# Maxima 11 instead of 13 steps ahead of the scores in a fused attention and mixture-of-experts layer

## Chip, cores and metric

The kernel runs on one core of one Trainium2 chip. Time is the device time of that core in microseconds (us), the median of several executions. Engines: PE (TensorE), DVE (VectorE), ACT (ScalarE), POOL (GpSimd) and SP (SyncE, which here issues DMAs).

## What is computed

Four batches of 1024 tokens with 128 channels pass through four residual blocks: a rotation with a code book (`_L0_attn_a_ref`), a mixture of experts, attention with 16 heads, and the mixture of experts again. The change lies in the attention and in the routing of the last block:

```python
def _mha(x, Wq, bq, Wk, bk, Wv, bv, Wo, bo):
    ...
    scores = jnp.einsum('bhsd,bhtd->bhst', q, k) / jnp.sqrt(jnp.asarray(D, x.dtype))
    w = jax.nn.softmax(scores, axis=-1)
    o = jnp.einsum('bhst,bhtd->bhsd', w, v)
...
    logits = jnp.einsum('btd,ed->bte', x, router_w)
    top_vals, top_idx = jax.lax.top_k(logits, K)
    ...
    out = jnp.einsum('nk,nkd->nd', w_f, y_sel)
...
    x = x + _L0_ffn_ref(_layernorm(x, axis=-1), ...)
    x = x + _L0_attn_b_ref(_layernorm(x, axis=-1), ...)
    x = x + _L0_ffn_ref(_layernorm(x, axis=-1), ...)
```

A head has 8 channels; the experts are 8, of which each token uses 2.

## The kernel before

The attention works on 16 groups: group G is batch b = G // 4 and four of its heads, g = G % 4. A group has 16 steps, so a score step s from 0 to 255 is G = s // 16, kk = s % 16. In a score step PE multiplies one tile of 128 keys with half of the queries (512) for four heads (`scores`, L2182), ACT takes the exponentials (L1195), and PE multiplies them with the values (`times_values`, L2223).

The softmax needs each query's largest score before the exponentials. It is found by a first pass over the same scores with keys and queries exchanged: in each step of maxima PE makes four products (`first_pass`, L2195) and DVE reduces them two at a time (`maxima`, L1710, two instructions a step). After 8 steps of maxima one half of a group's queries is complete. `merge_maxima` (L1722, L1724) combines and transposes them, POOL negates them and splits them in two parts (`minus_max`, L785 to L787), and SP stores them to DRAM and loads them into two rows of Q (`shift_queries`, L530 and L535), so that the second product already has its maximum subtracted. A half's first scores wait for that load (`q_shifted`).

The maxima run AHEAD = 13 steps ahead: in loop step s every engine does the maxima of step s + AHEAD and the scores of step s. The loop starts at s = -13 with maxima alone and its last 13 steps have scores alone. A half's maxima are complete, and merged, in the step with (s + AHEAD) % 16 equal to 7 or 15.

All engines follow an order written out by hand. PE, for one step: side work for ACT (`fill_for_act`), values, scores and first pass interleaved. PSUM banks pass between the engines in an order fixed by `bank_order`: three for ACT (`act_banks`) and two double banks for the maxima. Beside the main work, steps have side tasks fixed by G and kk:

- g = 2, kk 0, 2, 6, 8: projections of the next batch, which POOL splits (`split_out`) and SP stores and loads;
- g = 0 and 1, kk 10: a normalised block of a coming batch (`norm_block`, POOL, L730) is transposed by PE (L1842);
- kk 3: the finished group's output is transposed (L2144) and normalised by DVE (`normalise`, L1730, L1732);
- for batches 0 and 1, groups 5 to 7 and 9 to 11 also prepare the routing of the last block. POOL sums the LayerNorm statistics of the first half of a batch (`early_stats(b, 0)`) and of its second half (`early_stats(b, 1)`, L846 to L855, ends in tile ve). DVE waits for both at g = 1, kk 15, before `scale_piece` (L1212 and following).

POOL's order within a group G is also fixed:

```python
minus_max(G, 1)
...
if g < 2 and b < B - 1:
    norm_block(2 * b + 2 + g)
...
if 1 <= b <= EARLY and g == 1:
    early_stats(b - 1, 0)
early_sends(2 * (G - 2 * NG))
if G + 1 < GROUPS:
    minus_max(G + 1, 0)
if g < 2 and b < B - 1:
    low_part(2, 2 * b + 2 + g)
    bias_block(2 * b + 2 + g)
...
elif 1 <= b <= EARLY and g == 1:
    early_stats(b - 1, 1)
```

In group 0 eight gathers of expert results (L653) stand between `minus_max(0, 1)` and `norm_block(2)`.

In the last group (G = 15) no maxima are left after its third step, and batch 2 is routed there by `routed_late`: rows normalised by DVE, transposed by PE, router product, two largest, ranks, places, weights. From step LATE (kk 6 of the last group) ACT has a fourth bank. When attention ends, the experts of the last block start, and POOL scatters and gathers token rows (L644, L653).

Of the kernel before, what the change touches and what calls it, by code (L numbers as in the profile page):

```python
# [64 lines left out]
PAIRS = -(-RT // 2)  # L65

GROUPS = B * NG
AHEAD = 13
EARLY = 2
STEP0, STEP1 = -AHEAD, GROUPS * STEPS  # L70
ACT_BANKS = 3
# [28 lines left out]
def max_task(s):  # L100

    G, kk = divmod(s, STEPS)
    if G < 0:
        return None
    b, g = divmod(G, NG)
    if kk == 12 and G == GROUPS - 1:
        return "half", 0
    if kk == 3 and G:
        return "out", G - 1
    if g == 0 and b > 0 and kk in (13, 14):  # L110
        return "wo", b - 1, kk - 13
    if g == 2 and 1 <= b <= EARLY and kk == 15:
        return "logits", b - 1
    if g == 3 and 1 <= b <= EARLY and kk == 9:
        return "rank", b - 1
    return None


def bank_order():

    AR, DR = {}, {}
    for s in range(STEP0, STEP1):
# [5 lines left out]
        for i in range(2):  # L128
            if i == 1 and max_task(s):
                DR[max_task(s)] = len(DR)  # L130
            if s < STEP1 - AHEAD:
                DR["max", s, i] = len(DR)
# [3 lines left out]
def hybrid_layer(nc, a, out):  # L136
    AR, DR = bank_order()
    ctx = ExitStack()
    with ctx:
# [221 lines left out]
        def beside_index(f, b):  # L361

            return B + b - EARLY if f else b

        def rows_known(f, b, u):

            if f and b < EARLY:
                return G_("rows_early"), 2 * b + u + 1
            return G_("rows_ready"), 2 * (beside_index(f, b)) + u + 1
# [29 lines left out]
        def max_taken(*key):  # L399
            return G_("max_taken"), DR[key] + 1  # L400
# [13 lines left out]
        def rows_bank(f, b):  # L414

            return six[:, 3, :] if f and b < 3 else misc[:]

        def route_bank(f, b):
            return six[:, 0, :] if f == 0 and b == 0 else s1[:, 1, :]
# [555 lines left out]
        def _(act):  # L975
# [76 lines left out]
            def rows_out(f, b, u):  # L1052

                act.wait_ge(G_("rows_turned"), 2 * beside_index(f, b) + u + 1)
                if f or b:
                    act.wait_ge(G_("lgs_done"), beside_index(f, b))
                act.activation(hfs[:, u * BLK:(u + 1) * BLK], rows_bank(f, b), ACT.Copy).then_inc(G_("rows_stored"), 1)

            def second_weight(f, b):
                act.wait_ge(G_("d2_ready"), sparse_index(f, b) + 1)  # L1060
                act.activation(ed2[:], d2[:], ACT.Exp).then_inc(G_("ed2_ready"), 1)
# [72 lines left out]

            def routed_late(kk):

                if kk in (7, 8):
                    rows_out(1, 2, kk - 7)
                elif kk == 13:
                    second_weight(1, 2)  # L1140

            def attention_end(e):
# [65 lines left out]
        def _(dve):  # L1208
# [240 lines left out]
            def batch_top_two(f, b, parts=(0, 1, 2)):  # L1449
                if 0 in parts:  # L1450
                    if f:
                        dve.wait_ge(G_("places_early"), EARLY)
                    dve.wait_ge(G_("lgs_done"), beside_index(f, b) + 1)
                    link(dve.tensor_copy(lgb[:], route_bank(f, b)[:, 64:64 + TPB * E]
                                         .rearrange("p (t e) -> p t e", e=E)))
                    largest_two()
                if 1 in parts:
                    link(chosen_two())
                if 2 in parts:
                    mark_two().then_inc(G_("both_ready"), 1)  # L1460
# [23 lines left out]
            def batch_weights(f, b):  # L1484
                dve.wait_ge(G_("ed2_ready"), sparse_index(f, b) + 1)
                link(dve.tensor_scalar(eds2[:], ed2[:], 1.0, None, ALU.add))
                link(dve.reciprocal(pw[:, b, 0, :], eds2[:]))
                ins = dve.tensor_tensor(pw[:, b, 1, :], ed2[:], pw[:, b, 0, :], ALU.mult)
                if f == 0 and b >= 2:
                    ins.then_inc(G_("weights_ready"), 1)  # L1490
                else:
                    link(ins)

            def batch_places(f, b, parts=(0, 1)):

                if 0 in parts:
                    first_lines(f, b)
                if 1 in parts:
                    line_places(b)
# [73 lines left out]
            def rows(f, b):  # L1573
                if f == 0:
                    dve.wait_ge(G_("x1_ready"), 2 * b + 2)
                rows_stats(b, 0)
                link(rows_stats(b, 1))
                rows_scale()
                for u in range(2):
                    rows_apply(f, b, u)  # L1580
# [98 lines left out]

            def routed_late(kk):  # L1680

                if kk == 3:
                    dve.wait_ge(G_("rows_early"), 2 * EARLY)
                    rows(1, 2)
                elif kk == 8:
                    batch_top_two(1, 2)
                elif kk == 11:
                    batch_places(1, 2)
                elif kk == 13:
                    batch_weights(1, 2)  # L1690

            def attention_end(e):
# [13 lines left out]
            def maxima(s, i):  # L1706

                t, th = divmod((s + AHEAD) % STEPS, 2)
                dst = mxp[:, th, t, 0:HG:HG - 1] if i else mxp[:, th, t, 1:HG - 1]
                dve.reduce_max(dst, taken_slot("max", s, i).rearrange("p (a n) -> p a n", a=2),  # L1710
                               AX.X).then_inc(G_("max_taken"), 1)

            def merge_maxima(s, half):

                n = 2 * ((s + AHEAD) // STEPS) + half
                dve.wait_ge(*max_taken("max", s, 1))
# [91 lines left out]
            for s in range(STEP0, STEP1):  # L1808
                G, kk = divmod(s, STEPS)
                b, g = divmod(G, NG)  # L1810
                first = (s + AHEAD) % STEPS
                if s < STEP1 - AHEAD:
                    maxima(s, 0)
# [24 lines left out]
        def _(pe):  # L1838
# [97 lines left out]
            def turn_rows(f, b, u):  # L1936

                n = 2 * beside_index(f, b) + u
                pe.wait_ge(*rows_known(f, b, u))
                if u or b:  # L1940
                    pe.wait_ge(G_("rows_stored"), n)
                for i in range(TPK):
                    ins = pe.transpose(rows_bank(f, b)[:, i * P:(i + 1) * P], hbs[:, b, TPK * u + i, :], ident)
                ins.then_inc(G_("rows_turned"), 1)

            def router(bank, rows, first=0, last=TPB):
                for i in range(first, last):
                    ins = pe.matmul(bank[:, i * E:(i + 1) * E], rows[:, i * P:(i + 1) * P], rwf[:], start=True, stop=True)  # L1948
                return ins

            def batch_router(f, b, halves=(0, 1)):
                for u in halves:
                    pe.wait_ge(G_("rows_stored"), 2 * beside_index(f, b) + u + 1)
                    if u == 0 and (f or b):
                        pe.wait_ge(G_("dest_ready"), beside_index(f, b))
                    elif u == 0:
                        pe.wait_ge(G_("t_ready"), 1)
                    ins = router(route_bank(f, b)[:, 64:64 + TPB * E], hfs, TPK * u, TPK * (u + 1))
                if u:
                    ins.then_inc(G_("lgs_done"), 1)  # L1960
# [9 lines left out]
            def batch_rank(f, b, parts=(0, 1)):  # L1970
                if 0 in parts:
                    pe.wait_ge(G_("both_ready"), beside_index(f, b) + 1)
                    if f == 0 and b == 0:
                        pe.wait_ge(G_("tri_ready"), 1)
                ins = rank_lines(route_bank(f, b)[:, 128:128 + (TPB + 1) * E], parts)
                if 1 in parts:
                    ins.then_inc(G_("rank_done"), 1)
# [122 lines left out]

            def routed_late(kk):

                if kk == 6:
                    pe.wait_ge(*max_taken("max", STEP1 - AHEAD - 1, 1))
                if kk in (6, 7):
                    turn_rows(1, 2, kk - 6)
                if kk in (7, 8):
                    batch_router(1, 2, (kk - 7,))
                elif kk in (10, 11):
                    batch_rank(1, 2, (kk - 10,))  # L2110

            def attention_end(e):

# [44 lines left out]
            def free_bank(*key):  # L2158
                n = AR[key]
                if n == late_first:  # L2160
                    pe.wait_ge(*max_taken("out", GROUPS - 2))
                if n > late_first:
                    pe.wait_ge(G_("act_taken"), n - LATE_BANKS + 1)
                elif n >= ACT_BANKS:
                    pe.wait_ge(G_("act_taken"), n - ACT_BANKS + 1)
                return act_bank(n)
# [211 lines left out]
```

## Time and profile before

| | |
|---|---|
| median of 3 runs | 1103.66 us (1101.62 to 1105.91) |
| profiled execution | 1099.18 us, its span 1097.4 us |
| mean granted TensorE clock | 0.914 |
| PE, DVE, ACT, POOL busy | 84%, 81%, 67%, 44% of the span |
| first maxima, first exponential | 245.87 us, 283.82 us |
| last maxima end, last exponential ends | 907.40 us, 942.98 us |

The attention phase is the stretch from about 246 to 943 us. Times in the trace count from the first instruction. In the timelines a row gives start, duration, engine, line, operation, output and inputs, the number of instructions merged, and in brackets the engine's idle time just before with what ended it.

### The profile page before, as it was taken

The numbers are of one execution on the slowest core, as the hardware profiler recorded it, in microseconds if no ns is written. First come the engines' busy times: TensorE is split into PE (matmuls) and PEld (weight loads), VectorE is DVE, ScalarE is ACT, GpSimd is POOL, SyncE is SP. The second block draws the span as 40 slices with busy tenths as digits, with TensorE's granted clock in tenths as the row PEclk, the third lists the DMA queues.
The fourth block names the chain that finished last, engine by engine and source line by source line (L and its number), as shares of the span: only waits on it lengthen the run. The fifth ranks groups of instructions, "written<-read, shape, count | busy, mean of one in ns | idle before, by whom it ended". The sixth has DMA issues, their size and how long they took to land.

```text
span 1097.4 us, 23130 instructions
## 1 busy us (share of the span) xinstructions
PE 922.2 (84%) x8466; PEld 524.6 (48%) x8466; DVE 890.4 (81%) x1870; ACT 732.3 (67%) x1453; POOL 477.9 (44%) x703
## 2 busy tenths in 40 slices
PE   2862889855899999999999999999999999999650
PEld 1352889852334434443444443443444434699650
DVE  6478768639999999999989999989999994578342
ACT  3232355430599989889887989887889998645320
POOL 3026676655655556116501416631411211526674
PEclk9865899975699999999999999999999998999885
DMA  7351445472100222100221200131110001246452
GB/s 242 108 175 46 131 124 167 136 266 101 42 18 5 78 82 82 42 3 5 73 87 42 85 8 10 66 108 46 54 45 8 15 8 51 73 117 169 139 152 66
DMA packets 96497, 89.80 MB, mean 82 GB/s; under 512 B 17021, under 2 KB 79616, under 8 KB 96258
## 3 DMA queue, kind: packets, MB, share of 16 engines
q1 hardware_dynamic: 88194, 71.54, 20.6%
q0 software_dynamic: 8192, 16.79, 5.3%
q8 instruction: 69, 1.13, 0.4%
q14 instruction: 42, 0.34, 0.1%
HBM read 44.98 MB, written 43.25 MB: 80 GB/s over the span
## 4 chain that ended last, share of the span: by engine, by line
PE 37%; DVE 32%; POOL 10%; issue 8%; ACT 6%; DMA 5%; SPq 1%; DVEq 0%; POOLq 0%; ACTq 0%
DVE mxp L1710 23%; PE acc L2223 12%; PE six L2182 8%; POOL xs L644 4%; ACT PB L1195 3%; POOL hbs L653 3%; PE misc L2182 3%; PE six L2012 2%; DMA hbs<-yd,dest 1%; PE six L2195 1%; PE six L2144 1%; PE acc L2207 1%; PE six L1948 1%; DMA SC<-yd,dest 1%; ACT SC L1182 1%
## 5 line engine op out<-in xcount | busy, mean ns | idle before, releaser
L1710 DVE TENSOR_REDUCE mxp<-six 128x2 f32<-128x1024 f32 x512 | 589.2, 1214 | 26.6 <-PE six L2195 25.4
L1195 ACT ACTIVATE PB<-six 128x512 f32<-128x512 f32 x688 | 388.7, 598 | 52.3 <-PE six L2182 29.2
L2223 PE MATMUL acc<-PB,Vg 128*32 128x256 f32 x3920 | 316.2, 394 | 15.0 <-ACT SC L1182 15.0
L2195 PE MATMUL six<-K,Q 32*128 32x512 f32 x1024 | 265.3, 517 | 27.3 <-DVE mxp L1710 16.8
L2182 PE MATMUL six<-Q,K 32*128 32x512 f32 x688 | 275.5, 503 | 0.0
L1195 ACT ACTIVATE PB<-misc 128x512 f32<-128x512 f32 x336 | 201.0, 598 | 58.3 <-PE misc L2182 39.3
L2182 PEld LDWEIGHTS six<-Q,K 32*128 32x128 f32 x688 | 110.9, 185 | 150.1 <-ACT PB L1195 82.7
L2182 PE MATMUL misc<-Q,K 32*128 32x512 f32 x336 | 168.4, 501 | 0.0
L644 POOL DMA_INDIRECT xs<-hbs,dest x128 | 127.0, 992 | 77.7 <-DVE dest L1520 40.4
L2223 PEld LDWEIGHTS acc<-PB,Vg 128*32 128x32 f32 x3920 | 78.3, 108 | 134.2 <-issue 79.3
L1086 ACT ACTIVATE PB<-PB 128x512 f32<-128x512 f32 x96 | 58.6, 612 | 101.2 <-DVE PB L1548 100.1
L785 POOL TENSOR_SCALAR shifts<-mxt 128x32 fp32r<-128x32 f32 x32 | 9.4, 293 | 266.2 <-DVE mxt L1724 264.6
L2195 PEld LDWEIGHTS six<-K,Q 32*128 32x128 f32 x1024 | 97.8, 189 | 45.0 <-DVE mxp L1710 33.6
L1548 DVE TENSOR_SCALAR PB<-six 128x512 f32<-128x512 f32 x96 | 63.4, 665 | 67.6 <-PE six L2012 66.9
L653 POOL DMA_INDIRECT hbs<-yd,dest x96 | 92.0, 959 | 54.6 <-issue 46.9
L2012 PE MATMUL six<-VH,stage 128*128 128x128 f32 x736 | 102.2, 283 | 0.3 <-issue 0.3
L2182 PEld LDWEIGHTS misc<-Q,K 32*128 32x128 f32 x336 | 61.7, 184 | 67.7 <-ACT PB L1195 34.6
L2012 PEld LDWEIGHTS six<-VH,stage 128*128 128x128 f32 x736 | 93.6, 198 | 1.0 <-issue 0.5
L2027 PE MATMUL acc<-w2s,PB 128*128 x384 | 53.7, 286 | 2.4 <-ACT PB L1086 2.4
L2027 PEld LDWEIGHTS acc<-w2s,PB 128*128 128x128 f32 x384 | 49.7, 202 | 2.6 <-issue 2.6
L1564 DVE COPY stage<-w1s 128x256 f32 x184 | 46.6, 312 | 5.2 <-issue 3.6
L2027 PE MATMUL six<-w2s,PB 128*128 x352 | 46.9, 275 | 1.4 <-ACT PB L1086 1.4
(328 smaller groups left out, 988.8 us busy)
## 6 DMA issues: line engine op xcount, KB each, us to landing
yd<-PB SPq DMA_DIRECT2D x40, 256.0 KB
kq<-parts SPq DMA_DIRECT2D x16, 512.0 KB, 2.9
K<-kq SPq DMA_DIRECT2D x16, 512.0 KB, 3.7
Q<-kq SPq DMA_DIRECT2D x16, 512.0 KB, 4.6
xs<-turned SPq DMA_DIRECT2D x4, 1472.0 KB, 12.1
K<-xs SPq DMA_DIRECT2D x20, 256.0 KB, 4.5
Q<-xs SPq DMA_DIRECT2D x20, 256.0 KB, 4.0
kq<-parts SPq DMA_DIRECT2D x16, 256.0 KB, 3.5
```

The lines of the kernel that those rows point to most:

```text
L644: pl.indirect_dma_start(xs[b], bass.IndirectOffsetOnAxis(ap=dest[:, b, k, i:i + 1], axis=0), hbs[:, b, i, :], None).then_inc(G_(f"sent{b}{ ...
L653: pl.indirect_dma_start(lines_back[b][:, k, i, :], None, yd[b], bass.IndirectOffsetOnAxis(ap=dest[:, b, k, i:i + 1], axis=0)).then_inc(G_( ...
L1086: act.activation(sqs[:, n % 3, 0:w], rls[:, n % 2, 0:w], ACT.Square).then_inc(G_("sqp_done"), 1)
L1195: act.activation(PB[:, s % 3, j, :], scores, ACT.Exp).then_inc(G_("act_taken"), 1)
L1548: dve.tensor_scalar(rls[:, n % 2, 0:w], big[:, n % 3, 0:w], 0.0, None, ALU.max).then_inc(G_("rlp_done"), 1)
L1564: ins = dve.tensor_copy(stage[:, n % STAGED, i, :], w1s[:, ds(at, HID)])
L1710: dve.reduce_max(dst, taken_slot("max", s, i).rearrange("p (a n) -> p a n", a=2), AX.X).then_inc(G_("max_taken"), 1)
L2012: ins = pe.matmul(big[:, n % 3, at:at + P], stage[:, group % STAGED, r % TG, c * P:(c + 1) * P], hTs[:, group % 2, r % TG * P:(r % TG + 1) ...
L2027: ins = pe.matmul(result_bank(group)[:, r % TG * D:(r % TG + 1) * D], sqs[:, n % 3, at:at + P], w2f[:, ds(expert_at[b, r] + c * D, D)], st ...
L2182: pe.matmul(bank, K[rows, G % NG, t * P:(t + 1) * P], Q[rows, G % NG, u * BLK:(u + 1) * BLK], start=True, stop=True).then_inc(G_("act_fill ...
L2195: ins = pe.matmul(slot[:, c * BLK:(c + 1) * BLK], Q[rows, G % NG, t * P:(t + 1) * P], K[rows, G % NG, th * BLK:(th + 1) * BLK], start=True ...
L2223: ins = pe.matmul(acc[RB * j:RB * (j + 1), n], Vg[:, G % 2, t, j, :], PB[:, s % 3, j, n], start=(t == 0 and half == 0), stop=(t == TPB - 1 ...
```

## The change

AHEAD goes from 13 to 11. Each merge then happens two score steps later (kk 4 and kk 12 instead of kk 2 and kk 10), the loop begins at s = -11, and its last 11 steps have no maxima. Each piece of batch 2's routing in the last group moves one step later, on all engines. The first use of the fourth ACT bank, which lies in the maxima's banks, waits for the last maxima instead of for the output of group 14.

```diff
-AHEAD = 13
+AHEAD = 11
...
-                if kk in (7, 8):
-                    rows_out(1, 2, kk - 7)
-                elif kk == 13:
+                if kk in (8, 9):
+                    rows_out(1, 2, kk - 8)
+                elif kk == 14:
                     second_weight(1, 2)
...
-                if kk == 3:
+                if kk == 4:
                     dve.wait_ge(G_("rows_early"), 2 * EARLY)
                     rows(1, 2)
-                elif kk == 8:
+                elif kk == 9:
                     batch_top_two(1, 2)
-                elif kk == 11:
+                elif kk == 12:
                     batch_places(1, 2)
-                elif kk == 13:
+                elif kk == 14:
                     batch_weights(1, 2)
...
-                if kk == 6:
+                if kk == 7:
                     pe.wait_ge(*max_taken("max", STEP1 - AHEAD - 1, 1))
-                if kk in (6, 7):
-                    turn_rows(1, 2, kk - 6)
                 if kk in (7, 8):
-                    batch_router(1, 2, (kk - 7,))
-                elif kk in (10, 11):
-                    batch_rank(1, 2, (kk - 10,))
+                    turn_rows(1, 2, kk - 7)
+                if kk in (8, 9):
+                    batch_router(1, 2, (kk - 8,))
+                elif kk in (11, 12):
+                    batch_rank(1, 2, (kk - 11,))
...
                 if n == late_first:
-                    pe.wait_ge(*max_taken("out", GROUPS - 2))
+                    pe.wait_ge(*max_taken("max", STEP1 - AHEAD - 1, 1))
```

## Rows read from the trace of the kernel before

**Rows 1.** The page: span, then busy us, share and instructions of engines.
```profile
span 1097.4 us, 23130 instructions
...
PE 922.2 (84%) x8466; PEld 524.6 (48%) x8466; DVE 890.4 (81%) x1870; ACT 732.3 (67%) x1453; POOL 477.9 (44%) x703
```

**Rows 2.** Stretches of the attention phase, columns in the first line.
```profile
core 0: us, PE busy (x) PEld busy (x) DVE busy (x) ACT busy (x) POOL busy (x), PEclk, DMA share, GB/s
257.80:283.80 26.00, 13.46 (x36) 4.91 (x36) 25.35 (x53) 0.00 (x0) 12.49 (x17) 0.50 0.12 31
862.50:900.40 37.90, 36.65 (x400) 15.29 (x392) 37.73 (x39) 34.77 (x67) 6.28 (x11) 1.00 0.04 11
...
523.10:569.40 46.30, 44.19 (x430) 19.40 (x428) 40.68 (x52) 38.68 (x73) 16.40 (x25) 0.97 0.26 95
...
924.70:934.90 10.20, 10.20 (x44) 3.31 (x43) 3.57 (x33) 5.99 (x12) 0.00 (x0) 0.50 0.01 2
```

**Rows 3.** Timeline of all engines, 850 to 862 us: merge to first scores.
```profile
851.18 0.21 DVE L1724 STREAM_TRANSPOSE mxt<-mxc 128x32 f32<-128x32 f32 x1
...
851.32 11.36 DVE L1710 TENSOR_REDUCE mxp<-six 128x2 f32<-128x1024 f32 x10
...
852.20 0.29 POOL L787 TENSOR_SCALAR shifts<-mxr 128x32 fp32r<-128x32 f32 x1
...
852.51 0.52 SPq L530 DMA_DIRECT2D shift<-shifts  x1
...
854.55 1.04 SPq L535 DMA_DIRECT2D Q<-shift  x2
...
861.70 0.47 PE L2182 MATMUL misc<-Q,K 32*128 32x512 f32 x1
```

**Rows 4.** Timeline of ACT in the last group: exponentials on bank misc.
```profile
909.83 0.59 ACT L1195 ACTIVATE PB<-misc 128x512 f32<-128x512 f32 x1
...
914.68 0.60 ACT L1195 ACTIVATE PB<-misc 128x512 f32<-128x512 f32 x1
```

**Rows 5.** Chain of waits, 505 to 530 us (start, us, what).
```profile
511.24 0.22 DVE mxt L1724
...
512.54 1.24 POOL hTl L680
513.78 1.24 POOL x L738
515.01 0.70 POOL turned L846
...
523.42 0.21 POOL ve L855
523.65 0.18 DVE rs L1212
```

**Rows 6.** Timeline of DVE, 516 to 534 us: group 5, kk 15.
```profile
523.65 0.17 DVE L1212 TENSOR_SCALAR rs<-ve 128x8 int32<-128x8 int32 x1 [0.61 <-POOL ve L855]
```

**Rows 7.** Timeline of DVE, 683 to 698 us: group 9, kk 15.
```profile
693.81 0.17 DVE L1212 TENSOR_SCALAR rs<-ve 128x8 int32<-128x8 int32 x1 [0.62 <-POOL ve L855]
```

**Rows 8.** Timeline of PE, 516 to 534 us.
```profile
525.94 0.50 PE L2195 MATMUL six<-K,Q 32*128 32x512 f32 x2 [0.23 <-DVE mxp L1710]
```

**Rows 9.** Timeline of all engines, 302 to 310 us: a block is normalised and transposed.
```profile
302.73 3.14 POOL L730 TENSOR_SCALAR hb<-x,mv,rs 128x128 f32<-128x128 f32 x4
...
309.20 0.66 PE L1842 MATMUL six<-cst,hb 128*128 128x128 f32 x4
```

**Rows 10.** Stretches around a pause of PE after the attention phase.
```profile
1018.00:1020.40 2.40, 0.14 (x2) 0.00 (x0) 0.87 (x4) 1.12 (x2) 1.79 (x3) 0.99 0.16 55
1020.40:1027.40 7.00, 0.00 (x0) 0.00 (x0) 0.00 (x0) 0.00 (x0) 5.17 (x7) 0.50 0.35 107
1027.40:1030.60 3.20, 3.19 (x15) 3.19 (x16) 0.33 (x1) 0.60 (x1) 2.39 (x3) 0.50 1.04 273
```

**Rows 11.** Timeline of POOL, 955 to 982 us: the first gather of the last block.
```profile
979.74 1.00 POOL L653 DMA_INDIRECT hbs<-yd,dest  x1 [20.77 <-issue]
```

## The prediction

> **What bounds the kernel now.** I read the page first: DVE is busy for 81% of the span, PE for 84%, POOL for less than half [rows 1]. A mean over the span says little here, so the second view is the table of stretches. It shows three regimes of the attention phase [rows 2]. In the lead-in (257.8 to 283.8 us) there are no scores yet: DVE is busy 25.35 of 26.00 us and PE waits for it, at half clock. In a plain group (862.5 to 900.4) DVE is busy 37.73 of 37.90 us: it is the bound. In a group that also projects the next batch (523.1 to 569.4) DVE drops to 40.68 of 46.30 and PE has 44.19: there PE's order is the bound. The timeline gives the rate: ten reductions of maxima in 11.36 us [rows 3], so a step of two costs DVE 2.27 us. ScalarE needs less: between two exponentials on the bank misc nine of them lie in 914.68 - 909.83 = 4.85 us, 0.54 each, 2.16 us for the four of a step [rows 4]. So DVE sets the pace until the last maxima, ScalarE after them.
>
> Two counters matter below: k counts the steps of maxima, s the steps of scores. Program order ties them rigidly: s = k - 13 before, s = k - 11 after. Work whose place is given by G and kk goes with s; merges go with k.
>
> **Part 1, the shorter lead.** The order of the k steps on DVE is unchanged, and the scores start two steps earlier: 2 x 2.27 = 4.5 us sooner. If nothing else waits, this is kept to the end, where two steps without maxima go (2 x 2.16 = 4.3 us by ScalarE). Gain 4.3 to 4.5; I take -4.5, hidden nowhere, since the lead-in is all DVE.
>
> **Part 2, the way of the maxima into Q.** A merge must reach the Q rows before the half's first scores. In the place shown [rows 3] the transpose ends at 851.39, POOL's three operations at 852.49, the store is issued at 852.51, the two loads from 854.55. Store to load is 2.04 us; the second load is issued half of 1.04 later, and by the same 2.04 lands at 857.1. So the path takes 5.7 us. The scores came at 861.70, 10.3 us after the merge; less 4.5 that is 5.8. It fits by 0.1. In the other half of a group the normalisation at kk 3 now comes ahead of the merge instead of behind it, which takes away what made its window longer, so that window is of the same size. Bounds: 0, and 0.3 us at each of some 16 tight places, 4.8. I take 0.5, as the row itself fits.
>
> **Part 3, what POOL does between a merge and score-step work.** This is the part that decides. In groups 5 and 9 POOL runs the LayerNorm sums of the second half (early_stats) only after minus_max of the next group's first half, so it is tied to k; VectorE waits for them at kk 15, tied to s. The chain of waits shows it whole [rows 5]: transpose ends 511.46, POOL's negations, hTl from 512.54, the addition of the bias from 513.78, the sums from 515.01, ve ends at 523.63, VectorE goes on at 523.65. That is 12.2 us from merge to release, with no pause in it; POOL is late already, VectorE waited 0.61 us [rows 6]. The other place is its copy: wait 0.62 us [rows 7]. The merge moves from kk 10 to kk 12 while the wait stays at kk 15, so between the two there are three steps of maxima and not five: VectorE arrives 4.5 us sooner and finds the same 12.2 us. Each wait grows from 0.6 to 5.1 us, +4.5 us. Does anything absorb it? Queued behind it on VectorE are the maxima of the next group; PE waits for their banks and already had 0.23 us idle behind the present wait [rows 8], so its lead is spent; its in-order queue also holds the scores, so ScalarE runs dry. The group that follows is the projecting one, where PE has no idle time to give back [rows 2]. Bounds: 0 to +4.5 each; I take +4.5 twice, +9.0. Put otherwise: the first wait returns s to where it stood before the change, the second makes it 4.5 us late.
>
> **Part 4, a block of LayerNorm in group 0.** POOL normalises block 2 after minus_max(0, 1) and eight gathers, all tied to k: done at 302.73 + 3.14 = 305.87. PE transposes it at kk 10, at 309.20 [rows 9]. PE now comes at 304.7, 1.2 us too early. Bounds 0 (a slower start at half clock) and 1.2; I take +1.0. The other such pairs (the same transposes in groups 1, 5 and 9, the routing rows in groups 6 and 10, the splits of the projections) start right behind minus_max, without eight gathers before them, and have three steps or more of PE's and ACT's other work until their reader: 0.
>
> **Part 5, TensorE's clock.** Two pauses of 4 to 5 us are new for PE. In the only long pause after the attention phase PE did nothing from about 1018.1 us; the granted clock was 0.99 up to 1020.4, 0.50 from there to 1027.4, and still 0.50 for 3.2 us in which PE worked again [rows 10]: 1.2 instead of 2.4 GHz, which costs at most half of such a stretch, 1.6 us. Bounds 0 and 2 x 1.6; I take +1.5. The Trainium skill (TensorE: Matmul & The Clock Gate, Part 1) says that half rate is the default and activity lifts it; by this rule both pauses would bring the half clock and the term would be 3.2, by the clock of a plain group (1.00) it would be 0.
>
> **Part 6, routing of batch 2 one step later.** On VectorE rows(1, 2) follow the last merge directly, in time as before. On PE, POOL and ScalarE every piece keeps its distance to the next. Counted from the end of attention it is one step (2.2 us) later; behind it stands POOL's scatter of batch 2, which has 20.77 us idle before the first gather [rows 11], and the staging of weights, ready about when PE needs it. Cost 0, at most 0.5; without that cover 2.2. The wait for the first late bank changes its semaphore and is met two steps earlier: 0. The tail's half-clock stretch (10.2 us at 0.50 [rows 2]) may move by a step: +-2, in the range alone.
>
> **Sum** against the profiled execution (1099.18 us, span 1097.4, 4.5 below the median of the runs): -4.5 + 0.5 + 9.0 + 1.0 + 1.5 = +7.5, so 1106.7 there and 1111.2 for the median of 1103.66. I say 1111.
>
> **Rivals.**
> (a) The waits of part 3 cost nothing: the moved merge leaves them slack, or the projecting group swallows them. Place: kk 15 of groups 5 and 9; it decides if less than 2 us of each 4.5 reaches the end. Then -4.5 + 1.0 + 0.5 plus a rest of up to 2: 1100 to 1103, not slower. For it: 5.6 us of idle DVE time in the projecting group. Against: that idle time isn't PE's. Chance 0.13.
> (b) Only a part shows: one wait is absorbed, or no clock loss and no wait in group 0. Then +2 to +5.5: 1105 to 1109. Chance 0.27.
> (c) The way into Q is late too, by 0.5 us more than the row says, at nearly each of 30 boundaries: another 8 to 12 us, 1119 to 1123. Against: [rows 3]. Chance 0.07.
> (d) The change does what a shorter lead can do at most: nothing new waits, -4.5 with a better tail, 1097 to 1099. Chance 0.03.
> Forecast, two full waits: 0.50, its own range 1109 to 1115.
>
> **How the numbers follow.** 0.5% is 5.5 us, about what a measurement of this kernel can tell from no change. Below 1098.1: most of (d) and a little of (a), 0.04. Above 1109.2: the forecast but for its lower edge (0.47) and (c) (0.07), 0.54. Between: 0.42. The range reaches from (a) to the forecast's upper end: 1101 to 1116.
>
> **What the profile after would show.** First exponential near 279.3 us instead of 283.82. VectorE's wait for ve before the rsqrt guess about 5.1 us, twice, with POOL's chain still 12.2 us from the merge. A wait of PE for hb near 305. PE's first scores of a half at or just behind the landing of the shifts. End of attention 5 to 8 us later than 943. I am wrong if those two waits stay below 2 us, or if they are there and the end of the phase comes earlier all the same.

## The result

The changed kernel takes 1128.6 us (median of 5, 1122.07 to 1131.02), the kernel before 1101.62 us in the same comparison (1090.64 to 1105.91). The ratio is 1.0246, its 95% interval 1.0205 to 1.0287. So it is slower, as forecast, but by some 27 us instead of the 7.5 us of the sum, and beyond the range. The profiled execution took 1122.07 us, span 1120.3; the one of before had 1099.18 and 1097.4. The profiled run of the changed kernel is its fastest of five, so the profiles differ by 22.9 us and the medians by 27. The attention phase is 25.3 us longer and began 2.7 us earlier.

The page of the changed kernel, with the granted clock in the 40 slices. Each slice is 28 us; the phase lies in slices 9 to 35.

```profile
span 1120.3 us, 23130 instructions
...
PE 935.3 (83%) x8466; PEld 529.8 (47%) x8466; DVE 894.2 (80%) x1870; ACT 735.0 (66%) x1453; POOL 476.7 (43%) x703
...
PEclk9865999975899999999798999898999999999885
```

Against [rows 1] PE has 13 us more busy time for the same 8466 matmuls: part of the loss is work done at a lower clock. The stretches show where:

```profile
core 0: us, PE busy (x) PEld busy (x) DVE busy (x) ACT busy (x) POOL busy (x), PEclk, DMA share, GB/s
250.60:276.60 26.00, 13.47 (x36) 4.90 (x36) 25.35 (x53) 0.00 (x0) 12.75 (x17) 0.50 0.12 32
888.10:926.50 38.40, 37.15 (x400) 15.45 (x392) 37.89 (x39) 34.92 (x68) 6.26 (x11) 1.00 0.04 11
524.40:582.10 57.70, 49.15 (x435) 20.79 (x431) 42.61 (x53) 39.09 (x74) 20.61 (x34) 0.85 0.21 76
...
527.00:530.30 3.30, 0.03 (x1) 0.00 (x0) 0.35 (x1) 0.60 (x1) 2.74 (x9) 1.00 0.00 0
530.30:543.90 13.60, 10.27 (x59) 4.06 (x60) 9.76 (x12) 5.94 (x11) 2.04 (x3) 0.50 0.16 60
...
712.00:714.60 2.60, 0.00 (x1) 0.00 (x0) 0.00 (x0) 0.60 (x1) 2.13 (x7) 1.00 0.00 0
714.60:721.40 6.80, 4.19 (x27) 1.27 (x27) 5.55 (x9) 2.22 (x4) 4.64 (x7) 0.50 0.19 68
```

The first three answer to the first three of [rows 2]. Lead-in and plain group look as before. The projecting group took 57.7 us instead of 46.3: PE, which had been busy for all but 2.1 us of it, is idle for 8.5. The last four are the two pauses and what came behind them. PE stops (for 6.53 and 5.21 us by its timeline), and then its clock is 0.50 (1.2 GHz) for 13.6 us and 6.8 us.

Now the timeline of DVE around the two waits; they answer to [rows 6] and [rows 7]:

```profile
529.95 0.54 DVE L1212 TENSOR_SCALAR rs<-ve 128x8 int32<-128x8 int32 x1 [5.40 <-POOL ve L855]
...
714.93 0.17 DVE L1212 TENSOR_SCALAR rs<-ve 128x8 int32<-128x8 int32 x1 [5.42 <-POOL ve L855]
```

The chain of waits shows the same work of POOL as [rows 5], at the same length: 517.58 to 529.92 is 12.3 us.

```profile
517.58 0.22 DVE mxt L1724
...
518.87 1.24 POOL hTl L680
520.11 1.24 POOL x L738
521.35 0.70 POOL turned L846
...
529.72 0.20 POOL ve L855
```

PE's timeline: what was 0.23 us idle in [rows 8] is 6.53 us. In the second row eight products with the values follow at 1.08 us, ten microseconds later the same eight take 0.64.

```profile
533.55 0.79 PE L2195 MATMUL six<-K,Q 32*128 32x512 f32 x2 [6.53 <-DVE mxp L1710]
534.28 1.08 PE L2223 MATMUL acc<-PB,Vg 128*32 128x256 f32 x8
...
544.45 0.64 PE L2223 MATMUL acc<-PB,Vg 128*32 128x256 f32 x8
```

**Where the 22.9 us are.** I cut each trace at the first exponential of every group, and call the distance to the next group's the group's length. The lead is the distance from the first maxima to the first exponential, the phase runs from the first maxima to the last exponential's end. "Plain" is the sum of groups 1 to 5, 8, 9 and 12 to 14. The rows e1 to e11 are the experiments below, with their lead where it isn't 11 (e1, e3, e4, e9 and e10 have 11). All in us:

```
                      lead   G0  plain   G6    G7   G10   G11   G15  phase
before                38.0  38.8 398.8  46.4  43.2  46.1  43.5  42.6  697.1
after                 33.4  43.2 404.7  57.7  45.6  54.0  44.6  39.1  722.4
e1  later wait        33.8  41.9 404.8  46.3  43.9  49.2  43.8  39.1  702.8
e2  earlier wait, 13  38.0  40.1 414.2  46.9  43.5  46.8  43.1  38.8  711.3
e3  norm_block first  33.4  43.6 405.8  57.7  48.4  56.4  45.6  39.1  730.1
e4  e1 and e3         33.4  45.6 405.6  48.2  47.5  48.4  43.7  38.9  711.3
e5  12, later wait    35.7  46.6 404.1  48.1  44.7  48.7  43.8  38.5  710.2
e6  13, later wait    38.1  47.4 398.8  47.0  47.8  47.0  43.2  38.8  708.2
e7  13, routing later 38.0  40.1 398.8  47.3  47.7  46.0  43.5  38.1  699.5
e8  12                35.7  39.9 404.2  56.5  45.6  55.0  43.8  38.5  719.1
e9  out behind merge  33.4  42.5 402.7  46.6  47.9  50.8  48.8  46.0  718.8
e10 wait filled       33.4  43.7 407.1  52.5  43.3  52.4  43.4  39.0  715.1
e11 12, out behind    35.7  38.9 401.6  46.4  47.8  48.2  44.7  38.2  701.6
```

Before to after: lead -4.5 (37.95 to 33.43 before rounding), G0 +4.4, plain +5.9, G6 +11.3, G7 +2.4, G10 +7.9, G11 +1.1, G15 -3.5 (the rows round to +25.0 of 25.3). The gain in G15 isn't the change's: before had 10.2 us of half clock there [rows 2], and other profiles at AHEAD 13 without it have 38.1 to 38.8 too. The two groups with the waits lost 19.2 us where the waits had grown by 4.8 us each.

In the lead, the timeline of ACT shows the first exponential 7.2 us earlier than before; 4.5 of it is the lead, 2.7 an earlier start of the phase (243.18 instead of 245.87):

```profile
276.61 0.60 ACT L1195 ACTIVATE PB<-misc 128x512 f32<-128x512 f32 x1 [27.59 <-PE misc L2182]
```

In group 0 PE now waits for the normalised block (timeline of PE; [rows 9] had no wait), POOL finishes it at 305.03, and the clock drops behind that short pause too:

```profile
305.17 1.09 PE L1842 MATMUL six<-cst,hb 128*128 128x128 f32 x4 [2.05 <-POOL hb L730]
```

```profile
303.00:305.20 2.20, 0.15 (x5) 0.06 (x1) 1.41 (x2) 1.09 (x2) 2.03 (x3) 0.96 0.00 0
305.20:308.40 3.20, 3.20 (x24) 1.35 (x24) 0.33 (x1) 1.46 (x3) 0.00 (x0) 0.50 0.00 0
```

### The profile page after: what moved, and what is told of

Same layout as the page of the kernel before. It is cut to its first block, busy times and chain, and to the rows that moved or that the text cites. A ratio compares the mean times of both kernels' runs of the same rounds, so it can differ in the third digit from the quotient of the medians.

```text
span 1120.3 us, 23130 instructions
## 1 busy us (share of the span) xinstructions
PE 935.3 (83%) x8466; PEld 529.8 (47%) x8466; DVE 894.2 (80%) x1870; ACT 735.0 (66%) x1453; POOL 476.7 (43%) x703
## 4 chain that ended last, share of the span: by engine, by line
PE 37%; DVE 32%; POOL 12%; issue 9%; DMA 6%; ACT 4%; SPq 0%; DVEq 0%; POOLq 0%; ACTq 0%
DVE mxp L1710 24%; PE acc L2223 11%; PE six L2182 7%; POOL xs L644 4%; POOL hbs L653 3%; PE misc L2182 3%; PE six L2012 2%; DMA hbs<-yd,dest 2%; ACT PB L1195 2%; PE six L2195 1%; PE six L2144 1%; PE six L1948 1%; POOL SC L653 1%; PE acc L2027 1%; DMA xs<-hbs,dest 1%
## 5 line engine op out<-in xcount | busy, mean ns | idle before, releaser
L2223 PE MATMUL acc<-PB,Vg 128*32 128x256 f32 x3920 | 323.1, 402 | 13.6 <-ACT SC L1182 13.4
L2195 PE MATMUL six<-K,Q 32*128 32x512 f32 x1024 | 268.7, 524 | 37.7 <-DVE mxp L1710 28.7
L2182 PE MATMUL six<-Q,K 32*128 32x512 f32 x688 | 280.2, 508 | 0.7 <-ACT PB L1195 0.7
## 6 DMA issues: line engine op xcount, KB each, us to landing
xs<-turned SPq DMA_DIRECT2D x4, 1472.0 KB, 12.4
```

The source lines that it names most:

```text
L2182: pe.matmul(bank, K[rows, G % NG, t * P:(t + 1) * P], Q[rows, G % NG, u * BLK:(u + 1) * BLK], start=True, stop=True).then_inc(G_("act_fill ...
L2195: ins = pe.matmul(slot[:, c * BLK:(c + 1) * BLK], Q[rows, G % NG, t * P:(t + 1) * P], K[rows, G % NG, th * BLK:(th + 1) * BLK], start=True ...
L2223: ins = pe.matmul(acc[RB * j:RB * (j + 1), n], Vg[:, G % 2, t, j, :], PB[:, s % 3, j, n], start=(t == 0 and half == 0), stop=(t == TPB - 1 ...
```

## The experiments

My theory: the two waits with the half clock behind them are the loss, and the rest is group 0 and the narrow windows. Rivals: the windows into Q or the order of side tasks lose it all along the phase; the routing's step; the clock by itself. Ratios are against the kernel before, on the same chip. The edits are made to the changed kernel unless said otherwise.

**e1, the wait taken later.** DVE takes the statistics three steps later, at kk 2 of the next group; all else is as changed.

```diff
-                if g == 1 and kk == 15:
+                if g == 2 and kk == 2:
                     dve.wait_ge(G_("stats_summed"), 6 + 2 * b)
```

> The changed kernel (AHEAD 11) with one edit: VectorE's wait for POOL's LayerNorm sums and scale_piece 3 stand at g = 2, kk 2 instead of g = 1, kk 15, three steps later. Theory A (the two waits of 5.4 us, each with a stretch of half clock behind it, make most of the loss: the groups behind them took 11.4 and 7.9 us more than before): both waits vanish, no half clock right behind them, the phase is 17 to 20 us shorter than in the changed kernel, so 1.006 to 1.011 of the kernel before. Theory B (the waits cost their own 4.5 us each and the half clock has another reason): about 9 us shorter, half clock still there, 1.015 to 1.017. Theory C (the way into Q is what costs, the waits only take over its slack): within 3 us of the changed kernel.

Measured: 1107.6 us against 1099.96, ratio 1.0067 (1.0035 to 1.0099). In its timeline of DVE the instruction has no wait, and its stretch of the projecting group is 46.3 us again, as in [rows 2]:

```profile
531.69 0.38 DVE L1212 TENSOR_SCALAR rs<-ve 128x8 int32<-128x8 int32 x1
```

```profile
523.00:569.30 46.30, 43.79 (x436) 19.58 (x432) 41.05 (x49) 39.06 (x73) 21.40 (x37) 0.99 0.27 94
```

So 1.8% of the 2.5%, some 20 us, hang on those two waits. At the second place the edit has a cost of its own: the same DVE work now stands just before the normalisation, and PE is idle for 1.57 us at 706.1 with 3.4 us of half clock behind it.

**e2, the same wait alone.** The kernel before, with the wait two steps earlier.

```diff
-                if g == 1 and kk == 15:
+                if g == 1 and kk == 13:
```

> The kernel before (AHEAD 13) with one edit: the same wait two steps earlier, at g = 1, kk 13, so that it is three steps behind the merge as in the changed kernel. Nothing else of the change is in it. Theory A: both waits grow to about 5.2 us, half clock follows, 15 to 20 us slower than before (1.014 to 1.018). Theory B: about 9 us slower (1.008), no half clock. Theory C: within 3 us of before.

Measured: 1120.35 us, 1.0203 (1.0163 to 1.0243). The wait alone makes nearly the whole loss, with a lead of 13 and all windows wide. Timeline of DVE, and the stretches of the pause, of what follows, and of what follows that:

```profile
523.00 0.17 DVE L1212 TENSOR_SCALAR rs<-ve 128x8 int32<-128x8 int32 x1 [5.09 <-POOL ve L855]
```

```profile
518.00:523.60 5.60, 1.73 (x17) 0.69 (x13) 0.50 (x3) 2.29 (x5) 4.25 (x10) 1.00 0.00 0
523.60:533.80 10.20, 8.52 (x50) 2.80 (x50) 7.49 (x8) 4.54 (x8) 0.07 (x1) 0.50 0.00 0
533.80:540.00 6.20, 5.64 (x60) 2.31 (x56) 5.11 (x6) 5.21 (x10) 2.43 (x4) 1.00 0.35 131
```

The wait is 5.09 us, 4.5 longer than [rows 6], yet groups 5 and 9 grow by 7.6 and 7.7 us ("plain" has +15.4): each wait costs the 4.5 us by which it grew and 3 us more. Behind it PE has about half of the matmuls per microsecond that it has once the clock is back (50 in 10.20 us, 60 in 6.20).

**e3, the block of group 0 ahead of the gathers**, and **e4, e1 and e3 together.**

```diff
                 if G == 0:
+                    norm_block(2)
                     for i in range(2, 6):
...
-                if g < 2 and b < B - 1:
+                if G and g < 2 and b < B - 1:
                     norm_block(2 * b + 2 + g)
```

> The changed kernel with norm_block(2) of group 0 ahead of the eight gathers on POOL. Theory A (PE's wait for it, 2.05 us, and the half clock of 3.2 us behind it make group 0's loss of 4.4 us): group 0 3.5 to 4.5 us shorter, no wait of PE for hb, no half clock at 305 us, 1.020 to 1.022 of before. My prediction's size: 1.0 us. If group 0's loss is the way into Q: no change.

> The changed kernel with both edits (the wait three steps later, norm_block(2) first). Theory A: what is left of the loss is the way into Q at each half, 5.8 us from merge to first scores where the other work leaves a little less: 1 us or less a group, some 6 to 8 us in all, against 4.5 us gained at the start and about 4 at the tail's clock. So 1.000 to 1.006 of before. If the way into Q costs nothing: 0.992 to 0.996.

Measured: e3 1125.49 us, 1.0217 (1.0172 to 1.0262), profile phase 730.1 us; e4 1108.91 us, 1.0075 (1.0046 to 1.0103). Neither differs from its partner by more than the intervals. The profiles say why: group 0 has 43.6 and 45.6 us although the wait for the block is gone. The start of the scores runs at half clock for a time that differs between profiles, even among before, e2, e6, e7 and e12, whose code is the same up to the end of group 0 (9.5 to 34.0 us). With H the time from the first exponential to the end of that stretch:

```
                      H    G0               H    G0
before              9.5  38.8   after     11.3  43.2
e7  at 13          13.1  40.1   e1         7.8  41.9
e2  at 13          13.0  40.1   e10       13.1  43.7
e6  at 13          34.0  47.4   e3        21.8  43.6
e8  at 12          12.5  39.9   e4        27.0  45.6
e5  at 12          30.5  46.6   e9        17.7  42.5
e11 at 12           8.8  38.9   e12 at 13 23.5  44.0
```

The left column and e12, of kernels without that wait, lie within 0.4 us of one line, 0.35 us of group length per microsecond of half clock ((47.4 - 38.8) / (34.0 - 9.5)). After, e1 and e10, with the wait, lie 3.8, 3.7 and 3.6 us above it; e3, e4 and e9, at AHEAD 11 but without the wait, 0.5, 0.7 and 0.8 (e9 doesn't move the block; PE, slowed by the longer half clock, comes late enough). So the wait, with the half clock behind it, costs about 3 us. What the narrower windows cost here is under a microsecond and hardly clear of the line's own 0.4. The medians don't show that, as the spread of H is worth more.

**e5, a lead of 12 with the later wait**, and **e6, the kernel before with the later wait** (the edit of e1 made to the kernel before).

```diff
-AHEAD = 11
+AHEAD = 12
...
-                if g == 1 and kk == 15:
+                if g == 2 and kk == 2:
```

> AHEAD 12 instead of 11, with VectorE's wait three steps later as in e1. The way into Q now has 2.3 us more than the 5.8 us it takes. Theory A (in e1 the way into Q costs what the plain groups have lost: groups 1, 3, 4 and 5 0.8 to 1.3 us each, 13 and 14 0.4, some 6 us in all): every plain group is back at its length in the kernel before (group 1 38.2 us, group 5 38.4 or less), the lead-in is 2.3 us shorter than before, and the whole is 0.994 to 0.999 of the kernel before. Theory B (the plain groups lost it to the normalisation at kk 3 that now stands ahead of the merge, or to the clock): group 1 stays at 39.1.

> The kernel before (AHEAD 13) with VectorE's wait three steps later. The two waits of 0.6 us go. Theory A (a wait under 1 us is hidden by PE's lead and brings no half clock): within 1.5 us of before, 0.997 to 1.001. If even these short waits cost clock: 3 to 5 us faster.

Measured: e5 1108.46 us against 1104.84, 1.0015 (0.9978 to 1.0052); e6 1102.7 us, 0.9968 (0.9932 to 1.0004). The lead is 35.7 us in e5, half of the gain. But "plain" is 404.1, already 5.3 us more than before, and one step further, at 11 (e1), 404.8. So the loss in the plain groups isn't in proportion to the lead. The 0.6 us of wait that e6 takes away bring nothing in its groups 5 and 9 (38.3 and 38.4 us, before 38.4 and 38.3), so its median says little about them.

**e7, only the later routing.** The kernel before with `routed_late` one step later on all engines.

```diff
-                if kk == 3:
+                if kk == 4:
                     dve.wait_ge(G_("rows_early"), 2 * EARLY)
                     rows(1, 2)
...
-                if kk == 6:
+                if kk == 7:
                     pe.wait_ge(*max_taken("max", STEP1 - AHEAD - 1, 1))
...
```

> The kernel before (AHEAD 13) with batch 2's routing in the last group one step later and nothing else (the fourth bank still waits for the output of group 14, which at AHEAD 13 comes after the last maxima). Theory A: the routing is off the path, 0.998 to 1.002. If the half clock in the last group (10.2 us before, none after the change) hangs on where the routing stands, group 15 is 3 to 4 us shorter; if it comes and goes by itself (it was away in e2, which keeps the routing of before), it says nothing here.

Measured: 1099.35 us, 0.9952 (0.9919 to 0.9985). What follows the phase has 153.8 us there, 154.4 before and 154.7 after. The routing costs nothing. I don't count the small gain: e12, below, has the same routing and doesn't show it.

**e8, the changed kernel with a lead of 12.** The waits grow by about half as much.

```diff
-AHEAD = 11
+AHEAD = 12
```

> The changed kernel with AHEAD 12 and nothing else. VectorE arrives at its wait 2.27 us sooner than before, so both waits are 2.9 us. Theory A (wait plus half clock behind it once PE's pause is long): 2.3 us a place by the wait, and up to 3 more a place if the clock falls: 1.001 to 1.008 of before. If the wait is linear and the clock doesn't fall: -2.3 + 4.6 = +2.3 us, 1.002. If the loss of the changed kernel came from the way into Q: below 1.0.

Measured: 1120.52 us, 1.0158 (1.0113 to 1.0204), above all that I had expected. Timeline of DVE, and the stretches of pause and what follows:

```profile
525.23 0.54 DVE L1212 TENSOR_SCALAR rs<-ve 128x8 int32<-128x8 int32 x1 [3.19 <-POOL ve L855]
```

```profile
522.00:526.70 4.70, 2.53 (x20) 1.07 (x16) 1.44 (x4) 2.85 (x5) 4.02 (x10) 1.00 0.00 0
526.70:537.00 10.30, 8.08 (x50) 2.83 (x50) 7.92 (x9) 4.74 (x9) 1.01 (x2) 0.50 0.21 79
```

A wait 2.6 us longer than before (3.19, the other 3.20) costs 10.1 us in G6 and 8.9 in G10, hardly less than one 4.8 us longer (11.3 and 7.9). PE's own pauses were 4.28 and 2.97 us there, and 10.2 us of half clock came behind each. So the loss doesn't shrink in proportion to the wait; the drop of the clock is as long behind the shorter pauses.

**e9, the output's normalisation behind the merge.** At a lead of 11 the merge of a group's second half is at kk 4, and the normalisation at kk 3 is now ahead of it in DVE's queue. e9 is e1 with the normalisation at kk 5. **e11** does it at a lead of 12 (merge at kk 3, normalisation at kk 4).

```diff
-    if g == 0 and b > 0 and kk in (6, 9):
+    if g == 0 and b > 0 and kk in (7, 9):
         return "rows", b - 1, kk // 8
...
-    if kk == 3 and G:
+    if kk == 5 and G:
         return "out", G - 1
...
                 if n == late_first:
-                    pe.wait_ge(*max_taken("max", STEP1 - AHEAD - 1, 1))
+                    pe.wait_ge(*max_taken("out", GROUPS - 2))
```

(The same wait for group 14's output stands in `routed_late`. e11 has "out" at kk 4, AHEAD 12 and both waits, without the first hunk.)

> e1 (AHEAD 11, VectorE's wait three steps later) with the normalisation of the finished group moved from kk 3 to kk 5, behind the merge again as it was before the change (its readers, the transposes of the output rows, from kk 6 to kk 7; the two waits for the last maxima wait for the last normalisation). Theory A (the plain groups' 0.4 to 1.4 us each come from the normalisation ahead of the merge): group 14 back to 37.9, group 1 to 38.2 or 38.5, the phase 3 to 6 us shorter than e1, 1.001 to 1.004 of before. Theory B (they come from the narrow window of the way into Q): group 1 39.1 and group 14 38.3 as in e1, no gain.

> AHEAD 12, VectorE's wait three steps later, the normalisation at kk 4, behind the merge at kk 3. Nothing waits that did not wait before, and the lead-in is 2.3 us shorter. Theory A: plain groups at their length of the kernel before (38.2, 37.9), 0.995 to 0.999 of before, apart from what the half clock of the first group does by itself (38.8 to 47.4 us in the runs so far). If the plain groups stay 0.4 to 0.6 us longer as in e5: 0.999 to 1.002.

Measured: e9 1118.5 us against 1102.89, 1.0154 (1.0099 to 1.021); e11 1108.7 us, 1.0068 (1.0029 to 1.0108). The plain groups gain what I looked for: 404.8 to 402.7 at 11, 404.1 to 401.6 at 12. But e9 brings a wait of its own, in the last group, where PE's first late bank now stands behind a normalisation that is itself behind batch 2's rows in DVE's queue (timeline of PE):

```profile
935.04 0.79 PE L2182 MATMUL six<-Q,K 32*128 32x512 f32 x1 [4.99 <-DVE SC L1732]
```

G15 has 46.0 us for it, 6.9 more than after. That is the fault of my edit, and so its median isn't a verdict on the idea. e11 has no such wait, and its median still misses the 0.995 to 0.999 that I expected: 2.5 us less in the plain groups don't show in it against e5 (1.0015).

**e10, PE kept busy in the wait.** Before the first projection of groups 6 and 10 PE does the same three products six times more into the same bank; each overwrites the last, so nothing else changes. This leaves DVE's wait and takes PE's pause.

```diff
-                    project(*task[1:], free_bank(*task)).then_inc(G_("act_filled"), 1)
+                    bank = free_bank(*task)
+                    for _ in range(6 if task[2] == 0 and task[1] > 1 else 0):
+                        project(*task[1:], bank)
+                    project(*task[1:], bank).then_inc(G_("act_filled"), 1)
```

> The changed kernel with VectorE's waits left where they are, but TensorE repeats the first projection of groups 6 and 10 six more times (the same product into the same bank, some 0.65 us each at full clock, 4 us in all), work that falls into the pause. Both VectorE waits stay at 5.4 us. Theory A (the pause of PE is what lowers its clock, and the half clock behind it is more than half of the loss of groups 6 and 10): no half clock directly behind the wait or a short one, group 6 51 to 53 us instead of 57.7, group 10 50 to 52 instead of 54.0 or more, 1.012 to 1.017 of before although there is more work. Theory B (the wait itself makes the loss): groups 6 and 10 as long as in the changed kernel or longer, 1.024 or more.

Measured: 1122.21 us, 1.0203 (1.015 to 1.0256), profile phase 715.1. Timeline of DVE, then the stretches of the filled wait, of what follows it, and of the second wait:

```profile
531.88 0.17 DVE L1212 TENSOR_SCALAR rs<-ve 128x8 int32<-128x8 int32 x1 [5.44 <-POOL ve L855]
```

```profile
524.00:533.00 9.00, 9.00 (x62) 5.46 (x58) 3.39 (x9) 4.54 (x9) 6.69 (x18) 1.00 0.02 4
533.00:546.00 13.00, 11.36 (x119) 5.09 (x118) 12.20 (x12) 9.96 (x19) 2.36 (x3) 1.00 0.16 61
...
703.00:713.00 10.00, 8.84 (x61) 5.30 (x58) 4.39 (x9) 4.19 (x8) 8.48 (x17) 1.00 0.05 16
```

With the wait as long as after (5.44 us) the clock stays at 1.00, and in the 13 us behind it PE does 119 matmuls, where after did 59 in 13.6 us. G6 and G10 together have 104.9 us: 12.4 more than before (92.5), and 6.8 less than after (111.7), 9.2 less than e3 (114.1). So the waits by themselves cost at most 12.4 (the added products are in it). Against e1 and e4, which have the same lead without the waits (95.5 and 96.6), it is 9.4 and 8.3, about the 9.6 by which the waits grew. The half clock behind them costs 7 to 9. Groups 6 and 10 hold 28.3 us of half clock in the changed kernel, 35.9 in e3 and 6.7 in e10, so this is 0.3 us per microsecond, close to the 0.35 of group 0. The median is above the 1.012 to 1.017 that I expected, and its interval touches that of the changed kernel; the split rests on the profiles.

**e12, a lead of 13 with the later wait and the later routing**, the best of what the others left.

> The version that the runs so far point to: AHEAD 13 as in the kernel before, VectorE's wait three steps later (e6) and batch 2's routing one step later (e7). e6 and e7 gave 0.997 and 0.995 with intervals of 0.35% to each side. Theory A (both are off the path; their ratios are the spread of the clock in the kernel before): 0.997 to 1.001, group 5 and group 9 38.3 to 38.4, group 15 38 to 39. Theory B (each brings something): 0.990 to 0.995.

Measured: 1101.84 us against 1099.76, 1.0014 (0.9977 to 1.0051). No version found is faster than the kernel before; e12 has the edits of e6 and e7 and doesn't repeat their ratios below one.

## Why the prediction was right in sign and wrong in size

**Part 1, the lead: right.** 33.43 us against 37.95 is -4.5, as said, and the first exponential stands at 276.61.

**Part 2, the way into Q: window right, but a step that failed beside it.** The window closes to the microsecond. Timeline of all engines of the changed kernel, the place of [rows 3]:

```profile
881.34 0.21 DVE L1724 STREAM_TRANSPOSE mxt<-mxc 128x32 f32<-128x32 f32 x1
...
882.35 0.29 POOL L787 TENSOR_SCALAR shifts<-mxr 128x32 fp32r<-128x32 f32 x1
...
882.67 0.52 SPq L530 DMA_DIRECT2D shift<-shifts  x1
...
884.71 1.05 SPq L535 DMA_DIRECT2D Q<-shift  x2
...
887.34 0.47 PE L2182 MATMUL misc<-Q,K 32*128 32x512 f32 x1
```

From transpose's end to the scores it is 5.79 us; I had worked out 5.8 for the window and 5.7 for the path. So PE comes and just waits, and that costs little: one step less of lead at 12, with the normalisation and the wait where they are, costs the plain groups 0.7 us (e5 to e1). What I put at nothing was the other half of a group, with the normalisation now in front of the merge: 2.1 to 2.5 us (e1 to e9, e5 to e11). Together with 2.8 us that e11 still has over before (401.6 against 398.8), and whose cause I did not find, this is 5.9 instead of 0.5. The step that failed is the sentence that the normalisation ahead of the merge only takes away what made the window longer.

**Part 3, the two waits: right in place, mechanism and length, and nearly in size.** The waits are 5.40 and 5.42 us (said 5.1), POOL's chain 12.3 us (said 12.2), and PE has no time to give back. Their own cost is 12.4 us at most by e10 against before, and 9.4 by e10 against e1, where +9.0 was said.

**Part 4, the block in group 0: right, too small.** The wait is 2.05 us instead of 1.2, and with the half clock behind it costs about 3 (e3, e4, e9 against after, e1, e10 on the line of H), not 1.0.

**Part 5, the clock: the step that failed where it decided.** I took "still 0.50 for 3.2 us in which PE worked again" from one pause as the length of the effect, and half of it as its price. Behind the new pauses the granted clock was 0.50 for 13.6 and 6.8 us, in e2 for 10.2 us, in e8 for 10.3. The price was 7 to 9 us for both, not 1.5. At the place of [rows 10] matmuls of 128 rows followed the pause, here scores and maxima of 32 rows; that this makes the difference is not shown, and in group 0 it was 3.2 us as well. The Trainium skill (TensorE: Matmul & The Clock Gate, Part 1), that half rate is the default and activity lifts it, is borne out by the trace in that each of these pauses brought 0.50; that activity lifts it soon is not, as in e6 PE was busy for 34 us at 0.50. The 3.2 us came from the row and was no bound. Nor is the price in proportion to the wait: against e5, the same lead without them, the waits of 3.2 us in e8 cost 8.4 and 6.3 us (56.5 - 48.1 and 55.0 - 48.7).

**Part 6, the routing: right.** e7, and POOL still has 18.28 us idle before the first gather ([rows 11] had 20.77):

```profile
1002.16 1.00 POOL L653 DMA_INDIRECT hbs<-yd,dest  x1 [18.28 <-issue]
```

**The rivals.** (a), (b) and (d) fell: nothing absorbs the waits. (c), a way into Q late at nearly every boundary, happened in small: the plain groups lose 5.9 us, but, as far as the cause is known, by the order of DVE's queue (2.1 to 2.5) more than by the path (0.7), and e2 makes +2.0% with no narrow window at all.

The sum with the measured terms, against the profile: -4.5 + 5.9 + 9.4 + 3 + 7 = +20.8, where the phase has +25.3. What is left is 3.0 us that groups 6 and 10 have over before in e1 too (95.5 against 92.5) and G0's own half clock and window (4.4 - 3), while G7 and G11 (+3.5) and G15 (-3.5) cancel; that cancelling is luck, as both hang on half clock that comes and goes. Against the +7.5 said, the phase is 17.8 us longer: 5.5 by the clock term, 5.4 by the plain groups, 3.4 in group 0, 3.0 in groups 6 and 10, 0.4 by the waits. So Part 5 and Part 2 missed by about the same amount. Even all upper bounds together (-4.3 + 4.8 + 9.0 + 1.2 + 3.2 + 0.5 = +14.4) give a median of 1118; the bounds of the clock and of the plain groups were too low themselves.

**Open.** Why the clock stays at 0.50 for 8 to 34 us after the first scores, with PE busy without a break, is not settled. Two stretches of e6, the first after the start of the scores, the second a plain stretch later:

```profile
284.00:318.00 34.00, 33.92 (x220) 10.40 (x219) 25.83 (x24) 22.84 (x42) 14.12 (x18) 0.50 0.10 24
331.40:369.60 38.20, 36.95 (x400) 15.27 (x396) 37.84 (x39) 35.36 (x69) 19.43 (x29) 1.00 0.02 4
```

Half clock also comes without a pause. In all fourteen profiles it begins near the end of groups 6 and 10, during or right behind the router products (8 columns each), with PE idle for 1.1 us at most before it, and lasts 3.4 to 20.5 us. Where it is long it reaches far into G7 or G11, and G7 varies with it (43.2 to 48.4 us in the table, with 0 to 19 us of half clock). Why its length differs is open too. Timeline of PE before the first one of the kernel before, which begins at 566.4:

```profile
563.94 1.92 PE L1948 MATMUL six<-rwf,hbs 128*128 128x8 f32 x16 [0.58 <-ACT PB L1195]
```

Also open are 2.8 us of the plain groups, and what share of e10's 12.4 us is its added products.

## What to carry to other kernels

Where two counters run at a fixed distance, shortening it moves every wait between them; list, per wait, which counter the producer and which the consumer follows, and compare the distance with the length of the chain, before any gain of the shorter lead is counted. Price a new pause of TensorE like the ones here (2 to 6.5 us) at its length and the half clock behind it, which was worth 1 us in group 0 and 2 to 6 us at each of the other places, even where the pause was short. If the pause can't be avoided, try to move the wait to a point where the data are ready (here one line, worth 1.8%). A term measured at one place of the trace, such as the time at half clock, holds for the work that followed there; take the spread over all such places as its bound.

## What the runs showed of the hardware

- The half clock behind a pause lasted far longer than the pause: 0.50 for 13.6 us behind 6.53 us, 6.8 us behind 5.21 us (both in the changed kernel), 10.3 us behind 4.28 us (e8), and only 3.2 us behind 2.05 us in group 0. From the first scores to the end of the phase, all twelve pauses of PE of 2.04 to 6.53 us in the profiles brought 0.50, and two of the three of 1.40 to 1.57 us (e1 and e9, not e4).
- It can also last 34 us with PE busy for 33.92 of 34.00 us (e6), and 9.5 us in the kernel before, whose code is the same up to there: a spread worth about 9 us of 1100, 0.35 us per microsecond. A single execution can differ by that much without any change of the kernel.
- Filling PE's pause with products that are thrown away kept the granted clock at 1.00 through a 5.44 us wait of DVE (e10).
- The clock fell to 0.50 behind the router products of groups 6 and 10 in all fourteen profiles, without a long pause of PE, for 3.4 to 20.5 us.
